# Second and third phase of a three-phase language model kernel put in one block, third phase's steps in a new order, its gated low halves on GpSimd

## The reference

```
h = tower(x)                                   # phase 1: 4 layers of state space + hidden layer 1024, final layernorm
h = h + attention(layernorm(h))                # phase 2: 16 heads of 16, scores exp(-gamma * scale * |q-k|^2), causal
h = h + ffn(layernorm(h))                      # phase 3: 2 layers, each as follows
  qkv = shift(x) @ wqkv[l]                     # 8 heads of 64; q, k: l2norm, scale, rotary with xpos
  x = x + local_attention(q, k, v) @ wo[l]     # softmax over the window of 128 before
  h = layernorm(shift(x)); a, g = split(h @ w1[l] + b1[l])      # 2 x 682
  x = x + (a * gelu(g)) @ w2[l] + b2[l]
```

## Time and profile before

| | us |
|---|---|
| median of 3 runs | 1392.0 (1385.31 to 1448.82) |
| profiled execution | 1391.85, span 1390.1 |
| PE busy | 1252.5 (90%), x9057 |
| DVE / ACT / POOL busy | 1026.5 (74%) / 921.6 (66%) / 565.8 (41%) |
| granted TensorE clock, mean | 0.964 |

### The profile page before, as it was taken

How to read it: one execution, slowest core, us unless ns; L and a number is a source line. 1 busy time by engine, 2 the same in 40 slices (tenths; PEclk the granted TensorE clock), 3 DMA queues, 4 the chain that set the end, 5 groups by cost and what they waited for, 6 DMA issues and landing times. The chain is left out here.

```text
span 1390.1 us, 26419 instructions
## 1 busy us (share of the span) xinstructions
PE 1252.5 (90%) x9057; PEld 1070.5 (77%) x9057; DVE 1026.5 (74%) x2698; ACT 921.6 (66%) x2023; POOL 565.8 (41%) x601
## 2 busy tenths in 40 slices
PE   2799999999999985999847787999999999999987
PEld 2699899889989974777635566888888877888886
DVE  5867666766676738998656887888888888888744
ACT  2455765665675545899716677777877788777743
POOL 6423511452352224553324564436445455444320
PEclk9899999999999997999978999999999999999998
DMA  7300000010000001000040002000100000000010
GB/s 170 93 1 14 33 30 1 14 63 0 1 0 1 1 5 49 9 17 9 17 114 1 1 5 85 5 6 5 45 5 4 18 5 13 20 20 20 20 30 17
DMA packets 34880, 33.74 MB, mean 24 GB/s; under 512 B 11340, under 2 KB 31424, under 8 KB 34752
## 3 DMA queue, kind: packets, MB, share of 16 engines
q1 hardware_dynamic: 32416, 29.65, 6.9%
q0 software_dynamic: 768, 2.10, 0.9%
q10 hardware_dynamic: 1568, 0.30, 0.1%
HBM read 25.75 MB, written 4.19 MB: 22 GB/s over the span
## 5 line engine op out<-in xcount | busy, mean ns | idle before, releaser
L360 ACT ACTIVATE t_gf<-t_ps_f,t_fb_cur 128x512 f32<-128x512 f32 x128 | 87.9, 687 | 167.3 <-PE t_ps_f L280 164.5
L508 DVE TENSOR_TENSOR t_g_lo<-t_gf,t_g_hi 128x512 fp32r<-128x512 f32 x128 | 92.5, 724 | 82.7 <-ACT t_g_hi L362 81.7
L293 PE MATMUL t_ps_o<-t_w_hi,t_g_hi 128*128 128x256 f32 x512 | 145.8, 285 | 1.1 <-DVE t_g_lo L508 1.1
L295 PE MATMUL t_ps_o<-t_w_hi,t_g_lo 128*128 128x256 f32 x512 | 144.8, 283 | 0.0
L294 PE MATMUL t_ps_o<-t_w_lo,t_g_hi 128*128 128x256 f32 x512 | 144.8, 283 | 0.0
L1672 PE MATMUL w_ring<-w_nh,w_w_hi 128*128 128x256 f32 x384 | 114.1, 297 | 12.4 <-POOL w_w_lo L2347 5.4
L2357 POOL TENSOR_TENSOR w_m<-w_m 128x512 f32<-128x512 f32 x64 | 85.3, 1332 | 66.6 <-DVE w_m L2104 66.5
L644 POOL TENSOR_TENSOR t_rs<-t_ve,t_neghalf 128x4 f32<-128x4 f32 x32 | 38.2, 1194 | 181.1 <-DVE t_ve L469 179.6
L278 PE MATMUL t_ps_f<-t_nh,t_w_hi 128*128 128x512 f32 x256 | 104.0, 406 | 7.5 <-DVE t_nl L607 3.6
L1674 PE MATMUL w_ring<-w_nl,w_w_hi 128*128 128x256 f32 x384 | 109.5, 285 | 0.0
L1673 PE MATMUL w_ring<-w_nh,w_w_lo 128*128 128x256 f32 x384 | 109.4, 285 | 0.0
(11 more groups left out here) (290 smaller groups left out, 4360.9 us busy)
## 6 DMA issues: line engine op xcount, KB each, us to landing
t_raw<-in_L_tok_w SPq DMA_DIRECT2D x8, 1024.0 KB
out<-X SPq DMA_DIRECT2D x14, 256.0 KB
raw<-in_L_ffn_wqkv SPq DMA_DIRECT2D x2, 1536.0 KB, 7.4
raw<-in_L_ffn_w SPq DMA_DIRECT2D x4, 682.0 KB, 6.0
w_raw_o<-out SPq DMA_DIRECT2D x8, 256.0 KB, 2.8
w_xs<-X SPq DMA_DIRECT2D x16, 127.0 KB
w_raw<-in_L_ffn_w SPq DMA_DIRECT2D x2, 640.0 KB
t_raw_d<-in_L_tok_D SPq DMA_DIRECT2D x4, 256.0 KB
```

Source lines behind the costliest of these rows:

```text
L293: pe.matmul(out, g_hi[:, j % 4, tok], w2_hi[:, j, :], start=(j == 0 and t % 2 == 0), stop=False, skip_group_check=True)
L295: mm = pe.matmul(out, g_lo[:, j % 4, tok], w2_hi[:, j, :], start=False, stop=(j == FC - 1 and t % 2 == 1), skip_group_check=True)
L360: act.activation(gf[:, j % 2, :], ps_f[:, j % 2, :], ACT.Gelu, bias=fb_cur[:, j:j + 1]).then_inc(pf_free, 1)
L508: dve.tensor_tensor(g_lo[:, j % 4, :], gf[:, j % 2, :], g_hi[:, j % 4, :].bitcast(F32), ALU.subtract).then_inc(g_split, 1)
```

## The change

1. Phases 2 and 3 are in one block, with no barrier between. Each phase now returns its engines' lists, and `program` weaves them. Phase 3's small tiles, `raw_o`, `raw_2`, `tab`, `ident`, `mask`, `ah`, `al` and so on, are given space of their own (`window_opening`) for both phases.
2. Phase 3's small loads go to SP's queue at phase 2's start (`prefetch`: 22 small DMAs and, after the tables, `load_ow(0)`), its pads to DVE's start, its masks to POOL between half 1 and 2, its table to DVE after half 2. `load_1(0)` is issued once `wqkv` is split.
3. The third phase's first statistics, root, norm, turn, spread, split and first projection stand among phase 2's last halves. New waits keep them apart (`done`: stores of the tiles, clips, outputs).
4. The order inside phase 3's `half` is new on all engines: a half now begins later in the step, all projections of step m stand in half m+1, `rotate` of its first tile at the end of DVE's half m. `hi_1(0, 0)` stands before the gelus, `lo_1(0, 0)` in half 4 and `lo_2(0)` in half 5. Ring banks are renumbered (`RB`).
5. `hidden_lo` is on POOL, no more on DVE; its form and its six calls per step are the same.

```diff
+            with nc.Block() as block:
+                M2, M3 = 8, 16
...
+                def _(sp):
+                    store = a_sync(sp)
+                    prefetch, rest = w_sync(sp)
+                    prefetch()
+                    for s in range(M2 - 2):
+                        store(s)
+                    rest()
...
+                def _(pe):
+                    early_half = a_tensor(pe)
+                    half, turn_first = w_tensor(pe)
+                    for h in range(M2 + 1):
+                        early_half(h)
+                    early_half(M2 + 1, turn_first)
+                    half(1, lambda: early_half(M2 + 2))
+                    for h in range(2, M3 + 6):
+                        half(h)
...
+                def _(act):
...
+                    early_half(M2 + 5, lambda: spread(0, 0))
+                    early_half(M2 + 6)
+                    for h in range(1, M3 + 6):
+                        half(h)
...
+                def _(dve):
...
+                    pads()
+                    for h in range(M2 + 4):
+                        early_half(h)
+                        if h == 2:
+                            table()
+                    x0_variance(0)
+                    early_half(M2 + 4, lambda: x0_norm(0))
+                    split_in(0, 0)
+                    early_half(M2 + 5)
+                    rotate(0, 0, 0, 0)
+                    rotate(0, 0, 1, 1)
+                    x0_variance(1)
+                    x0_norm(1)
+                    fills()
+                    for h in range(1, M3 + 6):
+                        half(h)
...
+                def _(pool):
...
+                    for h in range(M2 + 4):
+                        early_half(h)
+                        if h == 1:
+                            masks()
+                    early_half(M2 + 4, lambda: x0_root(0))
+                    for h in range(M3 + 5):
+                        half(h)
...
@@ phase 2, DVE's half (norm_first is x0_norm(0)); PE's turn_first stands before values(c, 2), ACT's spread_first before output_hi(g, 0)
                     clip(f, 6, 3)
                     clip(f, 7, 0)
+                if norm_first:
+                    norm_first()
...
@@ phase 3, PE's half, first part in the new order
+                if real(g):
+                    hidden_in(g, 2, 0, 3, "a_full")
+                if real(d):
+                    values(NU * d + 0)
+                    turn_p(H * d + 3)
+                if real(b):
+                    project(b, 0, 0, 0, "q_full")
+                if last_output:
+                    last_output()
...
+                    hidden_in(g, 4, 0, 3, "a_full")
+                    hidden_out(g, 0, 1)
...
+                    scores(NU * c + 0)
+                    hidden_out(g, 1, 1)
+                    turn(0, 0, 0, "qs_full")
+                    hidden_out(g, 2, 1)
+                    if real(g):
+                        pe.wait_ge(S["gated"], FC * g + 6)
+                    project(b, 1, 1, 3, "k_full")
+                    turn_normed(f, 2)
+                    hidden_out(g, 3, 1)
+                    project_out(e, 0)
...
@@ phase 3, POOL
+            def hidden_lo(f, j):
+                pool.wait_ge(S["h_hi"], FC * f + j + 1)
+                pool.tensor_tensor(h_lo[:, j % HS, :], gate[:, j, :], h_hi[:, j % HS, :].bitcast(F32), ALU.subtract).then_inc(S["h_split"], 1)
...
+                if real(f):
+                    hidden_lo(f, 0)
+                if h == 5:
+                    lo_2(0)
+                if real(f):
+                    hidden_lo(f, 1)
...
                 if real(a):
                     add_sin(a, 0, 0)
                     add_sin(a, 0, 1)
+                if h == 7:
+                    lo_qkv(0)
+                if real(f):
+                    hidden_lo(f, 3)
+                    hidden_lo(f, 4)
+                    hidden_lo(f, 5)
+                if real(c):
+                    scale_p(NU * c + 3)
```

More of the change, by code:

```diff
@@ L999, in _, with scalar @@
             pe.wait_ge(s_pad, 1)
-            for h in range(M + 3):
-                half(h)
-        @block.scalar
-        def _(act):
+            return half
+        def scalar(act):
             def spread(s, b):
@@ new lines, in run @@
+            def run():
+                sp.wait_ge(done["qkv_l"], 8)
+                load_1(0)
+                last = slice(GT * (NG - 1), GT * NG)
+                sp.wait_ge(done["y_added"], NSQ)
+                sp.dma_start(out_v[:, last, :], X[:, last, :]).then_inc(S["h_out"], 16)
+                for stored in done["stored"]:
+                    sp.wait_ge(stored, 32)
+                sp.wait_ge(S["h_out"], 16)
+                shift(0)
+                shift(1)
+                load_qkv()
+                load_ow(1)
+                shift(2)
+                shift(3)
+                shift(4)
+                load_1(1)
+                shift(5)
+                shift(6)
+                shift(7)
+                load_h(8)
+                load_h(9)
+                shift(8)
+                load_h(10)
+                shift(9)
+                load_h(11)
+                shift(10)
+                store(8)
+                load_h(12)
+                shift(11)
+                store(9)
+                load_h(13)
+                shift(12)
+                store(10)
+                load_h(14)
+                shift(13)
+                store(11)
+                load_h(15)
+                shift(14)
+                store(12)
+                shift(15)
+                store(13)
+                store(14)
+                store(15)
+                sp.wait_ge(S["stored"], 16 * NSQ)
@@ L1806, in half @@
-                if real(b):
-                    pe.wait_ge(S["kt_done"], 2 * b + 1)
-                    pe.wait_ge(S["kscaled"], 2 * b + 2)
-                    turn(1, 1, 1, "ks_full")
-                if real(f):
-                    hidden_out(f, 1, 0)
-                if real(c):
-                    turn_p(H * c + 4)
-                if real(f):
-                    hidden_out(f, 2, 0)
-                if real(c):
-                    values(NU * c + 1)
-                if real(b):
-                    scores(NU * b + 0)
@@ L1837, in half, with turn_first, scalar @@
[L1837 to L1845 removed]
+            def turn_first():
+                pe.wait_ge(S["ident"], 2)
+                pe.wait_ge(done["relu"], H * (NSQ - 1) + 4)
+                turn_in(0, 0)
+            return half, turn_first
+        def scalar(act):
             def hi_o(l):
@@ L2325, in _ @@
-            ins.then_inc(S["tab"], 1)
-            dve.wait_ge(S["tab"], 1)
-            for h in range(M + 6):
-                half(h)
-        @block.gpsimd
-        def _(pool):
+                    gated(f, 2, 3)
+                    gated(f, 3, 3)
+                if real(c):
+                    soft(H * c + 7)
+                    turned_p(H * c + 3)
+                    output_lo(NU * c + 0)
+                if real(a):
+                    rotate(a, 0, 0, 0)
+                if real(c):
+                    turned_p(H * c + 4)
@@ new lines, in half, with pads @@
+                if real(a):
+                    rotate(a, 0, 1, 1)
+                if real(c):
+                    inverse_sums(NU * c + 3)
+                    output_lo(NU * c + 1)
+                    turned_p(H * c + 5)
+            def pads():
+                dve.memset(neghalf[:, :], -0.5).then_inc(S["padp"], 1)
+                dve.memset(b1_all[:, :, :, :], 0.0).then_inc(S["pad"], 1)
+                dve.memset(xs[0:1, :, :, :], 0.0)
+                for a in (ah, al):
+                    dve.memset(a[:, 1, 0:1].bitcast(F32), 0.0)
@@ new lines, in table @@
+            def table():
+                dve.wait_ge(S["vec"], 16 * NLOAD)
+                for l in reversed(range(L)):
+                    for i in range(2):
+                        for u in range(2):
+                            ins = dve.tensor_tensor(tab[:, l, 2 * i + u, :, :], tab[:, 0, 2 * i + u, :, :],
+                                                    scl[:, i, u, l * HD:(l + 1) * HD].unsqueeze(1).broadcast_to([P, 2, HD]), ALU.mult)
+                ins.then_inc(S["tab"], 1)
+                dve.wait_ge(S["tab"], 1)
@@ new lines, in fills, with gpsimd @@
+            def fills():
+                dve.wait_ge(done["y_full"], NSQ)
+                for w in (w1_hi, w1_lo):
+                    dve.memset(w[:, :, :, HID:HIDP].bitcast(F32), 0.0)
+                for w in (w2_hi, w2_lo):
+                    dve.memset(w[:, FC - 1, :].bitcast(F32), 0.0)
+                dve.memset(mx[:, :, :], 0.0).then_inc(S["fill"], 1)
+                dve.wait_ge(S["fill"], 1)
+            return half, pads, table, fills, x0_variance, x0_norm, split_in, rotate
+        def gpsimd(pool):
```

734 lines of the change are left out of this document (336 added, 398 removed).

## The result

The changed kernel takes **1366.9 us** (median of 4 runs, 1365.4 to 1369.6) against 1389.9 (median of 4); the ratio is 0.985, 95% interval 0.983 to 0.986. One of the four executions before, of 1448.8 us, was in the slower state and is not in the ratio; without it the difference of the medians is 21 us instead of 23. The forecast was 10.5. The profiled execution took 1366.5 us with a span of 1364.7, against 1391.85 and 1390.1.

A forecast was written before the change was run, and what follows sets the result against it. PE was taken to bound the steady halves, the chain through all engines the start. From 1391.85 us, +5 - 6 + 0 - 3.5 - 6 + 0 = -10.5 gave 1381 us; range 1363 to 1399, with 1 in 5 outside.

The forecast's parts named there:

- a: Phase 2's start: masks, table and the wait for small loads move into it, slower by 5 us (bounds 2 and 12).
- b: Boundary of phases 2 and 3: first rotation 17 us earlier, of which 6 us remain at step 2's q (bounds 3, 11).
- c: Rest of the fill, steps 3 to 5: same chain of waits in both orders, 0 within 4 us.
- d: First hidden layer's weights: PE's 5.42 us wait goes, 2 us come late next, faster by 3.5 us.
- e: Ten and a half steady halves: between 0 and 10.5 us of PE idle to be had, faster by 6 us.
- f: The drain: a chain with the same links in both orders, 0 within 3 us.
- the walk: Tracing the new order through boundary and fill with profiled durations: q of step 2 6 us nearer, later round 1.4 us longer.
- Both signs: Forecast wrong if the fill's rounds get shorter than 27 us or the steady half changes by over 1 us.
- my slower rival: Steady halves: low halves stuck in POOL's queue with three slots make PE wait, +26 us, 1413 us; chance 0.1.
- all of it comes: Whole kernel: small loads land in time, boundary, weights, steady idle and drain all give their most, 1365 us; chance 0.2.

The follow-up runs named there:

- two-blocks run: Changed kernel with phase 2 in a block of its own and phase 3's loads, masks, table, norm and first turn behind a barrier: 1379.0 us, ratio 0.990.
- the swap: Kernel before, with the gate weights' low part made ahead of the second feed-forward weights' low part on GpSimd in half 4: 1381.5 us, ratio 0.993.
- mended: Changed kernel with the second feed-forward weights' low split moved behind the scaling of two probabilities and three low halves in GpSimd's queue: 1361.9 us, ratio 0.980.
- the third run: Kernel before with only the six low halves moved to GpSimd, the first two behind the second tile's key scaling: 1386.0 us, ratio 0.998.

## Why the prediction was right or wrong

| step | forecast | measured |
|---|---|---|
| a, phase 2's start, at its last clip | +5 | +5.5 |
| b, from there to q of step 2 | -6 | -6.9 |
| c, from there to `turn_in(4)` | 0 | +2.0 |
| d, weights, to step 0's end | -3.5 | -8.3 |
| e, ten halves | -6 (10.5 halves) | -16.1 |
| f, drain | 0 | 0 |

Measured times count from the first DVE instruction of phase 2 (519.1 before, 517.1 after).

**a** was right, by its parts too. PE's first turn is 1.15 us later for a forecast of about 1.5. Against the phase's first statistics, which the pads put back by 0.6, the last clip comes at 172.9 us, before at 168.0. (Other executions with the same phase 2 lie between 171.9 and 174.0, and between 166.1 and 168.9.) Masks 1.6 us (526.79 - 525.16), table 1.71, DVE's wait 1.29 for a forecast of 2. SP issued its 22 loads in 14.6 us, between the two ends I had (9.5 and 19.9).

**b** was right, by the sign that it named, the distance to phase 2's last clip (687.14 before, 690.64 after). The first rotation is 19.6 us nearer to it (forecast 17), the second tile's 12.2 (11), q of step 1 8.7 (7.6) and q of step 2, at 755.98, 6.9 (6). That the first rotation starts at 703.99 where the walk wrote 703 is luck: the walk left out a, which the measured times hold. Between the two rotations 7.4 us are lost for a forecast of 6, and the norm is more than that difference: 3.27 instead of 1.38. Two of its subtractions ran beside GpSimd's sums and took 1.34 and 1.35 us each, the two behind them 0.40. The sentence from the Trainium skill's "GPSIMD Engine Reference", Key points, that I weighed for the steady halves names DVE instructions with two SBUF inputs or in a 2-port mode. The trace agrees that DVE stretches beside GpSimd, and the cost was in the fill; whether these one-tensor subtractions run in such a mode no run shows.

The two-blocks run prices the join differently, at 12 us: the new order without it reached step 0 4.9 us later than the kernel before. The forecast compared old order in two blocks with new order in one, and for that pair a small net is what was found. **c** is 51.9 us before and 53.9 after, within its bounds of 4; the walk had found 1.4 us more and I had put it at nothing. One half of the fill differs by 3 us among like executions, so these 2.0 say little.

**d** was mis-sized. From `turn_in(4)` to step 0's `add_output` it is 77.2 us before (811.3 to 888.5) and 68.9 after (809.9 to 878.8). The term held the wait of 5.42 less 2 for what is late next. By the swap alone the wait was worth 7.5 us over this stretch, 1.9 of it the clock, which I had priced at the boundary and not here. What is late next was the right thing (`scale_p` behind `lo_2`) at twice its size, 4.2 us for the 2, again with the clock (0.96 in that half, 1.00 once mended). So the two errors cancel, by luck: 7.5 - 4.2 = 3.3 for the 3.5. The remaining 4.9 us of the 8.3 come from the new order's other halves before step 0 (from `turn_in(4)` to `turn_in(5)` it is 31.1 us, in the old order without the wait 34.7), though the turn stands at different places of a step in the two orders. The forecast had for them only c's nothing and the half of e beyond ten, and no run took a single part of them: their cause stays open.

**e** is the step that failed: "PE's own 37.3 stay, its products being the same. So between 0 and 10.5 are to be had". The bound was false: drawn busy time was taken for time that the products need. Products of before at the `gated` wait:

```profile
1056.07 0.28 PE L1685 MATMUL w_ring<-w_w_lo,w_h_hi 128*128 128x256 f32 x1
1056.19 0.28 PE L1686 MATMUL w_ring<-w_w_hi,w_h_lo 128*128 128x256 f32 x1
1057.41 0.50 PE L1592 MATMUL w_ring<-qkv_hi,w_ah 128*128 128x512 f32 x1 [0.94 <-DVE w_gate L2192]
```

Such a product starts 0.12 us after the last and is drawn 0.28 long, so its drawn end covers 0.16 us of the wait: 1.22 - 0.12 = 1.10 are lost, 0.94 are shown. The rest was not idle on any page. I summed the spacing of starts by function, up to the next group's first start, in one half of 38.26 us before, one of 36.60 after and one of 36.99 of the run with the old order and the low halves ahead of the key scaling. The 36 products of the projections take 8.90, 8.76 and 8.77 us: 0.13 is a wait under drawn ends, and it goes with the low halves' move. The 24 products of `project_out` take 2.99, 2.81 and 2.99, the same with and without the move: that is the order. In the old order they stand behind transposes, with 0.20 us to the second start and 0.117 between the others; in the new one behind `hidden_out`, all 0.113 apart. Turns and output steps give another 0.2 in this way. So of the 1.66 us that a half lost, 1.27 are DVE's waits (0.94 of them shown) and 0.39 is spacing that depends on what stands next to what. The 37.3 of the forecast held 0.7 us of both kinds. At most 37.0 us are needed in the old order and 36.6 in the new one, so 17 us were to be had in ten and a half halves, and the change had 16.1 in ten.

Taking only 6 of the range was the second half of the error. It rested on the fear that an order leaves new waits; the runs say that with DVE relieved hardly any is left (4.1 us in ten halves), and that without it they come at once (38.3 to 38.9). Both signs that the prediction gave for being wrong came: the half changed by 1.6 us, over 1, and one round of the fill took 25.5, under 27. What decides is the pair. In us a half:

| low halves on | VectorE | GpSimd, behind a late key scaling | GpSimd, behind nothing late |
|---|---|---|---|
| old order | 38.2 | 38.1 | 37.0 |
| new order | 38.9, 38.3 | not run | 36.6 |

In the changed kernel the first low half stands behind `scale_k` as well, but there it is not late: over the 69 low halves from 880 to 1290 us GpSimd waits 46.5 us, all of it for ScalarE's high half. GpSimd's queue was my slower rival. A low half stuck in that queue is real (the third run shows it with the first low half behind `scale_k`, at 1.1 us a half against the exchanged order), only not in the changed kernel.

The rival *all of it comes* gave 1365, and the time fell on it, though not by its terms: it had a at +3, the boundary at 11 and the drain at 3, none of which came, 5.4 from the weights, where the stretch gave 8.3, and 10.5 from the halves, where 16 did. The range held the time by luck too. The terms' bounds, taken as independent (root of the sum of squares), make 9 us down and 12 up, not the 14 of the prediction; from 1381 that would be 1372 to 1393, and the measured time lies below.

## What to carry to other kernels

A busy share that is read from drawn durations is no floor for a pipelined engine: take the spacing of starts in an undisturbed group, and look at every larger spacing, whether it is shown as idle or not. Some of it is wait; some belongs to the order and stays until the order changes. A wait on the engine that bounds the kernel is priced with the clock behind it (here 7.5 us for 5.4, and 4.2 for 2.6). When work moves to an engine with room, its place in that engine's queue decides whether the move counts: ask for each instruction ahead of it what that one waits for.

## What was not expected of the hardware

Of four 128x256 subtract-and-multiply operations on VectorE, with one tensor operand and two scalars each, the two beside GpSimd's 128x512 sums took 1.34 and 1.35 us, the two behind them 0.40; in the kernel before all four took 0.41. GpSimd's low half took 0.74 us, between the 0.61 and the 0.83 that the prediction weighed; VectorE's took 0.42. The granted clock was 0.50 from 855 to 857 us after a wait of only 2.62 us, while the same kernel's other waits of up to 1.9 us between 883 and 1256 left it at 1.00. In the fill, executions of like kernels differ by 3 us in the half from `turn_in(1)` on (26.6 to 30.0), of which the half ahead of it gives back up to 1.6, and in the drain by 4 (110.4 to 114.7), with no edit that would explain it; that stays open.
